# GpSimd's column sums before its squares, four result buffers, and two more maxima passes under the heads, in a fused attention and ternary-FFN kernel

## The chip, the cores and the metric

The kernel runs on one core of a Trainium2 chip. The metric is the device time of one launch in microseconds (us). One launch handles all eight sequences, weights included, from HBM to HBM.

## What is computed

Eight sequences of 512 tokens with 512 features pass through two sublayers. Cut to what matters:

```python
x = x + layernorm(attention(layernorm(x)))       # 16 heads of 32, causal, rope over the head index, softmax * 512**-0.5
x = x + layernorm(ffn(layernorm(x)))
def ffn(x):                                      # bitlinear: layer norm, then weights sign(round(w / mean|w|)) * mean|w|
    h = gelu(bitlinear(x, w_fc))                 # 512 -> 2048
    return bitlinear(h, w_proj)                  # 2048 -> 512; its layer norm needs mean and variance of h over 2048
```

The second bitlinear normalises h, row by row, over its 2048 hidden values. The kernel does this behind the product: it needs, for each token, the sum of the gelu values and the sum of their squares.

## The kernel before

**Steps.** The program is written out by hand, engine by engine, with semaphores (no scheduler). Step j (`iteration(j, prev, here, nxt, setup)`) overlaps three batches: the FFN of batch j-1 (`prev`), the attention of batch j (`here`), and the projections of batch j+1 (`nxt`). Steps 1 to 6 are "usual" and have all three; step 7 has no `nxt`; step 8 has only `prev`; step 0 prepares. Every engine runs its list strictly in order, so a wait holds all that stands behind it on that engine.

**Up phase.** TensorE (PE) makes 16 blocks of hidden values, 128 hidden features each, over 512 tokens (`up(u)`, L491). ScalarE (ACT) takes the gelu twice (L826, L827), VectorE (DVE) subtracts to get a low half (`hidden_low`, L1119); the block then stands as two f16 tiles, hT HI and hT LO. Between them stand passes of maxima (`max_pass`, L536, four matmuls with 1280 columns in all; `maxima` on DVE, L1124): one pass per head of the attention gives the row maxima for the softmax. `MAX_AT` puts ten passes in the up phase of their own step, `STEP_MAX` puts six in the heads of the step before.

**Sums.** `hidden_sums(u)` (L501, matmuls at L507) follows two blocks behind: eight matmuls of one column against ones add the block's gelu values over partitions into columns 264 to 267 of the PSUM bank `pv`. GpSimd (POOL) makes the squares in `squares(u)` (L1507): hi + lo (L1521), times itself (L1523), added to `acc` (L1526), block by block. `square_sums` (L513, matmuls at L518) adds `acc` over partitions with four matmuls in float32 (eight records), ahead of the weighing of head 6 (`SQUARES_AT`).

**Down product.** `ffn_down(tb, part)` (L522, L531) is the second product for 128 tokens (tb) and a quarter of the hidden values (part), eight matmuls of 512 columns. All of tb 0 comes ahead of the heads, (1, 0) behind the weighing of head 0, the others by `DOWN_AT` inside the heads.

**Heads.** In head h PE makes, in this order, queries and keys of the next batch (`QK_AT`, L487), pieces of the down product, `scores(h + 1)` (L554), a maxima pass where `STEP_MAX` has one, and `weigh(h)` (L581, 20 matmuls at L594), the product of probabilities and values. ACT takes exponentials (L868, L870), DVE their low half (`probs_low`) and `head_output(h)` (L1259: L1264, L1266, L1271). `weigh(h)` waits for the low halves of head h and for `pv` to be read (`pv_drained`).

**Finish.** For each tb DVE takes the down product out of PSUM (`final`, L1198) into one of two buffers `xn[:, tb % 2, :]`, makes moments, POOL raises to the power -1/2 (`power`, L1497), ACT normalises (`final` on ACT, L873, at the heads of `FINISH_AT`), POOL adds the residual (`finish`, L1541), SyncE stores. `hidden_mean` (L1177) and `hidden_variance` (L1185) on DVE read the two sums from `pv`.

Behind the heads comes the tail (attention's output projection, its layer norm, the turned inputs of the next up phase).

## Time and profile before

| | |
|---|---|
| median of 3 runs | 1301.1 us (1300.71 to 1302.18) |
| the profiled execution, its own time | 1301.28 us |
| its span (first to last instruction) | 1299.5 us |
| PE busy | 1183.3 us (91%) |
| DVE busy | 996.2 us (77%) |
| ACT busy | 763.5 us (59%) |
| POOL busy | 563.7 us (43%) |
| mean granted TensorE clock | 0.97 |

The time of the profiled execution is 1.8 us more than its span; sums below are made against 1301.28 us. The usual steps repeat to a hundredth of a microsecond: the first `up` of step 3 starts at 511.61 us and that of step 4 at 659.20 us, a period of 147.59 us. Times in the rows are counted from the start of the span. A row of the timeline stands for one or more like instructions in a row; its start is the start of the first.

### The profile page before, as it was taken

The page shows a single profiled execution, that of the slowest core. Times are in us where ns is not written, and L with a number is a line of the kernel's source. Part 1 is how long each engine was busy: PE and PEld are TensorE (multiplying, and loading weights), DVE is VectorE, ACT ScalarE, POOL GpSimd, SP SyncE. Part 2 cuts the span into 40 slices and gives each one's busy share as a digit, 9 for nine tenths or more (in the row PEclk, how much of TensorE's full clock was granted, in tenths as well). Part 3 has the DMA queues.
Part 4 walks back from the last instruction along what each step waited for, and adds up shares of the span by engine and source line. Part 5 has one row for each costly group of instructions (what it writes and reads, how often), then busy time and mean ns, then how long its engine had stood idle before and what let it go on. Part 6 is the DMA issues. An engine that isn't in the chain of part 4 may idle for free.

```text
span 1299.5 us, 24731 instructions
## 1 busy us (share of the span) xinstructions
PE 1183.3 (91%) x9300; PEld 647.9 (50%) x9300; DVE 996.2 (77%) x2892; ACT 763.5 (59%) x1406; POOL 563.7 (43%) x630
## 2 busy tenths in 40 slices
PE   6867789999999999999999999999999999988697
PEld 5224444555545554555545554555545554555343
DVE  4587977968787887968887887968888787867634
ACT  4628645666466755666465755666466754576390
POOL 1150603961269213971259312971159412881250
PEclk9896889999999999999999999999999999998899
DMA  8340221012300231012300222002300212000100
GB/s 333 73 154 2 50 82 34 2 25 66 106 1 3 58 89 51 2 26 66 106 1 2 58 63 77 1 20 68 110 1 3 56 43 66 1 3 18 49 1 32
DMA packets 47613, 65.08 MB, mean 50 GB/s; under 512 B 8548, under 2 KB 33156, under 8 KB 46086
## 3 DMA queue, kind: packets, MB, share of 16 engines
q1 hardware_dynamic: 47494, 63.51, 16.5%
q8 instruction: 73, 1.20, 0.4%
q14 instruction: 46, 0.38, 0.1%
HBM read 29.63 MB, written 8.39 MB: 29 GB/s over the span
## 4 chain that ended last, share of the span: by engine, by line
PE 52%; DVE 32%; ACT 11%; issue 3%; POOL 3%; DMA 0%; DVEq 0%; POOLq 0%; ACTq 0%
PE gen L487 19%; PE down L531 15%; DVE score L1139 8%; PE pv L594 4%; DVE hT L1031 4%; PE score L557 4%; DVE probs L1031 2%; PE gen L548 2%; DVE gen L1139 2%; PE score L569 1%; POOL rstd L1497 1%; DVE mx L1139 1%; DVE qkn L1244 1%; DVE bn L1170 1%; ACT qkn L808 1%
## 5 line engine op out<-in xcount | busy, mean ns | idle before, releaser
L1497 POOL TENSOR_TENSOR rstd<-veps,mhalf 128x1 f32<-128x1 f32 (+1 forms) x104 | 67.0, 645 | 501.8 <-DVE veps L1219 355.0
L868 ACT ACTIVATE probs<-score 128x512 f16<-128x512 f32 x360 | 189.2, 526 | 117.6 <-PE score L557 117.6
L487 PE MATMUL gen<-x2T,t1T 128*128 128x512 f16 x1024 | 241.9, 381 | 4.0 <-ACT x2T L807 2.5
L1031 DVE TENSOR_TENSOR probs<-score,probs 128x512 f16<-128x512 f32 x360 | 199.3, 595 | 51.3 <-ACT score L870 51.0
L531 PE MATMUL down<-t2T,hT 128*128 128x512 f16 x960 | 220.7, 381 | 0.2 <-DVE xn L1203 0.2
L870 ACT ACTIVATE score<-score 128x512 f32<-128x512 f32 x360 | 191.9, 533 | 0.0
L487 PE MATMUL gen<-xT,wa 128*128 128x512 f16 x768 | 181.9, 389 | 4.3 <-DVE mx L1139 4.3
L1031 DVE TENSOR_TENSOR hT<-gen,hT 128x512 f16<-128x512 f32 x160 | 108.4, 685 | 63.7 <-ACT gen L827 25.2
L487 PEld LDWEIGHTS gen<-x2T,t1T 128*128 128x128 f16 x1024 | 95.2, 98 | 108.9 <-ACT x2T L807 5.2
L826 ACT ACTIVATE hT<-gen,gam 128x512 f16<-128x512 f32 x128 | 88.0, 688 | 95.8 <-PE gen L487 95.7
L1139 DVE CUSTOM_DVE_ANT_0 score<-score,mask_rows 128x512 f32<-128x512 f32 (+3 forms) x312 | 143.1, 520 | 0.0
L531 PEld LDWEIGHTS down<-t2T,hT 128*128 128x128 f16 x960 | 90.5, 98 | 98.9 <-issue 2.3
L1526 POOL TENSOR_TENSOR acc<-acc,acc_add 128x512 f32<-128x512 f32 x105 | 133.2, 1268 | 8.2
L1521 POOL TENSOR_TENSOR acc_add<-hT 128x512 f32<-128x512 f16 x105 | 121.3, 1155 | 14.5 <-POOL acc L1526 0.4
L487 PEld LDWEIGHTS gen<-xT,wa 128*128 128x128 f16 x768 | 73.1, 100 | 89.9 <-issue 9.6
L1523 POOL TENSOR_TENSOR acc_add<-acc_add 128x512 f32<-128x512 f32 x105 | 109.3, 1041 | 8.2
L594 PE MATMUL pv<-v_sb,probs 128*128 128x65 f16 x2560 | 101.3, 195 | 9.6 <-DVE oA L1266 9.6
L594 PEld LDWEIGHTS pv<-v_sb,probs 128*128 128x128 f16 x2560 | 95.8, 99 | 17.6 <-DVE probs L1031 13.4
L487 PE MATMUL gen<-wa,xT 128*128 128x512 f16 x384 | 91.7, 388 | 3.7 <-DVE mx L1139 3.7
L1139 DVE CUSTOM_DVE_ANT_0 gen<-gen,mask_rows 128x512 f32<-128x512 f32 x200 | 91.8, 521 | 0.0
L557 PE MATMUL score<-qk 98*128 98x128 f16 x840 | 89.9, 246 | 0.0
L827 ACT ACTIVATE gen<-gen,gam 128x512 f32<-128x512 f32 x128 | 84.1, 657 | 0.0
(146 smaller groups left out, 1782.8 us busy)
## 6 DMA issues: line engine op xcount, KB each, us to landing
qk<-qkn SPq DMA_DIRECT2D x360, 64.0 KB, 2.0
xo<-x SPq DMA_DIRECT2D x8, 1024.0 KB, 5.4
hT<-x SPq DMA_DIRECT2D x8, 1024.0 KB, 6.4
out<-xn SPq DMA_DIRECT2D x32, 256.0 KB, 2.2
hT<-w_fc SPq DMA_DIRECT2D x4, 1024.0 KB, 15.8
hT<-w_down SPq DMA_DIRECT2D x4, 1024.0 KB, 5.5
t2T<-w_qk SPq DMA_DIRECT2D x2, 1024.0 KB, 8.5
probs<-w_v SPq DMA_DIRECT2D x1, 1024.0 KB, 10.8
```

The costliest lines, as they stand in the source:

```text
L487: mm = nc.tensor.matmul(bank[:, :], a, b, start=(start and n == 0), stop=(stop and n == len(pairs) - 1))
L531: mm = nc.tensor.matmul(bank[:, :], hT[:, half, u, PARTS * tb:PARTS * (tb + 1)], t2T[:, u, :], start=(u == 0 and half == HI), stop=(u == F ...
L557: return nc.tensor.matmul(bank[:, at:at + t1 - t0], qk[0:98, 1, h, PARTS * s:PARTS * (s + 1)], qk[0:98, 0, h, t0:t1], start=start, stop=Tr ...
L594: mm = nc.tensor.matmul(pv[:, VW * tb:VW * (tb + 1)], probs[:, h % 2, half, at:at + PARTS], v_sb[:, s, h, :], start=(s == 0 and half == HI ...
L826: nc.scalar.activation(hT[:, HI, u, :], bank[:, :], ACT.Gelu, scale=gam[:, 0:1])
L868: nc.scalar.activation(probs[:, h % 2, HI, 512 * i:512 * i + n], bank[:, 0:n], ACT.Exp, scale=1.0 / S_UP)
L870: nc.scalar.activation(bank[:, 0:n], bank[:, 0:n], ACT.Exp, scale=1.0 / S_UP).then_inc(exp_full, 1)
L1031: return V.tensor_tensor(out, whole, hi, ALU.subtract)
L1139: op = V.tensor_tensor_reduce(part, part, mask_rows[:, T - n:T], 1.0, -3.0e38, ALU.add, ALU.max, mx[:, TB * u + tb:TB * u + tb + 1])
L1521: P.tensor_tensor(whole[:, :], hT[:, HI, u, :], hT[:, LO, u, :], ALU.add).then_inc(sq_step, 1)
L1523: P.tensor_tensor(whole[:, :], whole[:, :], whole[:, :], ALU.mult).then_inc(sq_step, 1 if u else 2)
L1526: P.tensor_tensor(acc[:, :], acc[:, :], acc_add[:, :], ALU.add).then_inc(sq_step, 1)
```

## The change

It does the following in the steps with `prev` and `here` (1 to 7). Step 8 keeps `hidden_sums` and the old `squares`.

1. PE's `hidden_sums` is left out. POOL adds hi and lo of each block and adds that to a new tile `acc_sum`; the first two blocks are also squared in passing (`BOTH`). The squares of the other 14 blocks come behind the last sum, and need hi + lo once more. In place of `hidden_sums` stands `value_sums`: four float32 matmuls of `acc_sum` against ones, ahead of the weighing of head 0, which wait for all of POOL's sums.
2. `square_sums`, `hidden_variance` and the first two `final_terms` move from head 6 to head 12; the finishing of tb 0, 1 and 2 on ACT from heads 6, 9 and 13 to 13, 14 and 15.
3. Four result buffers instead of two (`result`: xn 0, xn 1, acc_sum, acc_add), each with its own semaphore; stores stand later in SyncE's list.
4. Piece (0, 3) of the down product goes behind `scores(1)`, ahead of the weighing of head 0; (1, 0) goes from behind that weighing to head 5.
5. Eight maxima passes in the heads (7 to 14) instead of six (8 to 13), eight in the up phase instead of ten. This holds for step 0 too.

```diff
-DOWN_AT = {0: [(1, 0)], 5: [(1, 1), (1, 2)], 6: [(1, 3)], 9: [(2, 0), (2, 1)], 10: [(2, 2), (2, 3)],
+DOWN_AT = {0: [(0, 3)], 5: [(1, 0), (1, 1)], 6: [(1, 2), (1, 3)], 9: [(2, 0), (2, 1)], 10: [(2, 2), (2, 3)],
            13: [(3, 0), (3, 1)], 14: [(3, 2), (3, 3)]}
-LAST_DOWN_AT = {h: [divmod(n + 4, 4)] for n, h in enumerate((0, 1, 2, 4, 7, 8, 9, 10, 12, 13, 14, 15))}
+LAST_DOWN_AT = {h: [divmod(n + 3, 4)] for n, h in enumerate((0, 1, 2, 3, 4, 7, 8, 9, 10, 12, 13, 14, 15))}
-SQUARES_AT = 6
-FINISH_AT = {6: 0, 9: 1, 13: 2}
+SQUARES_AT = 12
+FINISH_AT = {13: 0, 14: 1, 15: 2}
-STEP_MAX = {8: 0, 9: 1, 10: 2, 11: 3, 12: 4, 13: 5}
+STEP_MAX = {7: 0, 8: 1, 9: 2, 10: 3, 11: 4, 12: 5, 13: 6, 14: 7}
-MAX_AT = {0: 6, 2: 7, 3: 8, 5: 9, 7: 10, 8: 11, 9: 12, 10: 13, 11: 14, 12: 15}
+MAX_AT = {0: 8, 2: 9, 3: 10, 5: 11, 7: 12, 9: 13, 11: 14, 12: 15}
...
-        SQ_STEPS = 3 * FC
+        BOTH = 2
+        SUM_STEPS = 2 * FC + BOTH
+        SQ_STEPS = SUM_STEPS + 3 * (FC - BOTH)
...
+                def value_sums():
+
+                    pe.wait_ge(sq_step, SQ_STEPS * (j - 1) + SUM_STEPS)
+                    for tb in range(TB):
+                        mm = nc.tensor.matmul(pv[:, H_SUM + tb:H_SUM + tb + 1], acc_sum[:, PARTS * tb:PARTS * (tb + 1)],
+                                              ones32[:, 0:1], start=True, stop=True)
+                    mm.then_inc(hsum_full, 1)
...
                     need(pe, pv_drained, HEADS * j + h)
+                    if prev and here and h == 0:
+                        value_sums()
                     if prev and here and h == SQUARES_AT:
                         square_sums()
...
-                        if u >= 2:
+                        if u >= 2 and not here:
                             hidden_sums(u - 2)
...
+                def square_added(n):
+
+                    pool.wait_ge(sq_step, n)
+                    P.tensor_tensor(acc_add[:, :], acc_add[:, :], acc_add[:, :], ALU.mult).then_inc(sq_step, 1)
+                    pool.wait_ge(sq_step, n + 1)
+                    P.tensor_tensor(acc[:, :], acc[:, :], acc_add[:, :], ALU.add).then_inc(sq_step, 1)
+
+                def sums(u):
+
+                    n = SQ_STEPS * (j - 1) + 2 * u + (BOTH if u >= BOTH else 0)
                     pool.wait_ge(g_drained, g0 + G["up", u] + 1)
...
+                    P.tensor_tensor(acc_add[:, :], hT[:, HI, u, :], hT[:, LO, u, :], ALU.add).then_inc(sq_step, 1)
                     pool.wait_ge(sq_step, n + 1)
...
+                    P.tensor_tensor(acc_sum[:, :], acc_sum[:, :], acc_add[:, :], ALU.add).then_inc(sq_step, 1)
+                    if u < BOTH:
+                        square_added(n + 2)
...
                 for u in range(FC if prev else 0):
-                    squares(u)
+                    if here:
+                        sums(u)
+                    else:
+                        squares(u)
                     if nxt and u == 2:
                         power(LX, slice(0, TB), j + 2, j + 2)
+                for u in range(BOTH, FC if prev and here else 0):
+                    squares(u)
```

How the lists change at three places. First PE in a usual step, from the last blocks of the up phase to the weighing of head 0 (`up` writes gen<-x2T,t1T; the sums are pv<-ones; scores are score<-...; weighing is pv<-v_sb,probs). Before:

```order
L487 MATMUL gen<-x2T,t1T 128x512 x8
L507 MATMUL pv<-ones,hT 128x1 x8
L482 MATMUL gen<-ident,xn 128x128 x4
L531 MATMUL down<-t2T,hT 128x512 x16
L507 MATMUL pv<-ones,hT 128x1 x16
L569 MATMUL score<-mask_b,identb 128x512
...
L531 MATMUL down<-t2T,hT 128x512 x16
L569 MATMUL score<-mask_b,identb 128x512
...
L594 MATMUL pv<-v_sb,probs 128x65 x20
L531 MATMUL down<-t2T,hT 128x512 x8
```

Now:

```order
L500 MATMUL gen<-x2T,t1T 128x512 x16
L495 MATMUL gen<-ident,xn 128x128 x4
L554 MATMUL down<-t2T,hT 128x512 x16
L592 MATMUL score<-mask_b,identb 128x512
...
L554 MATMUL down<-t2T,hT 128x512 x8
L592 MATMUL score<-mask_b,identb 128x512
...
L554 MATMUL down<-t2T,hT 128x512 x8
L530 MATMUL pv<-ones,acc_sum 128x1 x4
L619 MATMUL pv<-v_sb,probs 128x65 x20
```

The sums have gone from between the blocks to one place right ahead of the weighing of head 0. Then POOL at the start of a step's blocks. Before:

```order
L1521 TENSOR_TENSOR acc<-hT 128x512
L1523 TENSOR_TENSOR acc<-acc 128x512
L1521 TENSOR_TENSOR acc_add<-hT 128x512
L1523 TENSOR_TENSOR acc_add<-acc_add 128x512
L1526 TENSOR_TENSOR acc<-acc,acc_add 128x512
L1521 TENSOR_TENSOR acc_add<-hT 128x512
L1523 TENSOR_TENSOR acc_add<-acc_add 128x512
```

Now:

```order
L1569 TENSOR_TENSOR acc_sum<-hT 128x512
L1571 TENSOR_TENSOR acc<-acc_sum 128x512
L1576 TENSOR_TENSOR acc_add<-hT 128x512
L1578 TENSOR_TENSOR acc_sum<-acc_sum,acc_add 128x512
L1559 TENSOR_TENSOR acc_add<-acc_add 128x512
L1561 TENSOR_TENSOR acc<-acc,acc_add 128x512
L1576 TENSOR_TENSOR acc_add<-hT 128x512
L1578 TENSOR_TENSOR acc_sum<-acc_sum,acc_add 128x512
```

From block 2 on two operations a block lead to the sums, and three more a block follow behind all sums. Last DVE in head 12, after the change:

```order
L1231 SCALAR_TENSOR_TENSOR acc_sum<-c_sum,h_negm,down 128x512
L1218 TENSOR_TENSOR h_msq<-h_negm 128x4
L1220 SCALAR_TENSOR_TENSOR h_var<-pv,h_msq 128x4
L1223 TENSOR_SCALAR e_fin<-h_var,c_fin 128x4
L1247 TENSOR_TENSOR veps<-mv,e_fin 128x1 x2
L1158 COPY wait_copy<-mhalf 128x1
L1165 ISA gen,mx<-gen,mask_rows 128x512
```

The variance, which waits for the weighing of head 12 itself, now stands ahead of that head's maxima; before, it stood in head 6, which has no maxima.

## Rows read from the trace of the kernel before

**Rows 1.** The page: the chain that ended last, by engine

```profile
PE 52%; DVE 32%; ACT 11%; issue 3%; POOL 3%; DMA 0%; DVEq 0%; POOLq 0%; ACTq 0%
```

**Rows 2.** Timeline of PE, up phase of step 3: start us, us, instruction

```profile
525.18 0.35 PE L507 MATMUL pv<-ones,hT 128*128 128x1 f16 x8
525.39 0.70 PE L548 MATMUL score<-qk 96*128 96x512 f16 x4
525.93 1.89 PE L487 MATMUL gen<-x2T,t1T 128*128 128x512 f16 x8
```

**Rows 3.** Timeline of POOL, blocks 0 to 3 of step 3

```profile
517.03 1.15 POOL L1521 TENSOR_TENSOR acc<-hT 128x512 f32<-128x512 f16 x1 [7.78 <-DVE hT L1031]
...
519.51 1.15 POOL L1521 TENSOR_TENSOR acc_add<-hT 128x512 f32<-128x512 f16 x1
520.74 1.04 POOL L1523 TENSOR_TENSOR acc_add<-acc_add 128x512 f32<-128x512 f32 x1
521.85 1.27 POOL L1526 TENSOR_TENSOR acc<-acc,acc_add 128x512 f32<-128x512 f32 x1
523.27 1.15 POOL L1521 TENSOR_TENSOR acc_add<-hT 128x512 f32<-128x512 f16 x1
...
526.99 1.02 POOL L1497 TENSOR_TENSOR rstd<-veps,mhalf 128x4 f32<-128x4 f32 x1
...
528.25 1.15 POOL L1521 TENSOR_TENSOR acc_add<-hT 128x512 f32<-128x512 f16 x1
```

**Rows 4.** Timeline of PE, step 3: weighing of heads 0, 6, 7, 8, 11, 12

```profile
560.61 0.77 PE L594 MATMUL pv<-v_sb,probs 128*128 128x65 f16 x20
...
586.54 1.02 PE L518 MATMUL pv<-ones,acc 128*128 128x1 f32 x8 [0.16 <-issue]
587.43 0.76 PE L594 MATMUL pv<-v_sb,probs 128*128 128x65 f16 x20
...
591.39 0.78 PE L594 MATMUL pv<-v_sb,probs 128*128 128x65 f16 x20
...
596.45 0.77 PE L594 MATMUL pv<-v_sb,probs 128*128 128x65 f16 x20
...
612.73 0.77 PE L594 MATMUL pv<-v_sb,probs 128*128 128x65 f16 x20
...
618.26 0.77 PE L594 MATMUL pv<-v_sb,probs 128*128 128x65 f16 x20
```

**Rows 5.** Timeline of DVE, step 3: heads 1, 6 and 14

```profile
569.96 1.28 DVE L1271 TENSOR_TENSOR xo<-oA,r_sum 128x128 f32<-128x128 f32 x1
...
588.23 0.16 DVE L1190 TENSOR_TENSOR h_msq<-h_negm 128x4 f32<-128x4 f32 x1 [1.39 <-PE pv L594]
...
588.96 1.61 DVE L1031 TENSOR_TENSOR probs<-score,probs 128x512 f16<-128x512 f32 x3
...
629.45 0.69 DVE L1031 TENSOR_TENSOR probs<-score,probs 128x512 f16<-128x512 f32 x1 [1.29 <-ACT score L870]
```

**Rows 6.** One DVE line, whole run: ns minimum, median, maximum

```profile
L1271 DVE TENSOR_TENSOR xo<-oA,r_sum x128: 292/293/1394, 117.1 to 1205.4; 128x128 f32<-128x128 f32 x128
```

**Rows 7.** Windows in step 7: busy us (count) of PE, PEld, DVE, ACT, POOL; PEclk

```profile
1163.80:1167.30 3.50, 1.91 (x28) 1.40 (x28) 3.37 (x7) 3.50 (x9) 2.32 (x3) 0.85 0.01 2
1167.30:1170.70 3.40, 2.37 (x20) 2.27 (x20) 2.01 (x6) 2.23 (x6) 0.00 (x0) 0.50 0.00 0
1170.70:1174.10 3.40, 3.40 (x24) 1.67 (x22) 2.54 (x9) 0.81 (x1) 0.74 (x3) 0.65 0.00 0
```

**Rows 8.** Timeline of PE, step 7: weighing of head 0, square sums, head 12

```profile
1147.23 0.78 PE L594 MATMUL pv<-v_sb,probs 128*128 128x65 f16 x20
...
1168.46 1.84 PE L518 MATMUL pv<-ones,acc 128*128 128x1 f32 x8 [1.03 <-DVE probs L1031]
...
1193.81 0.77 PE L594 MATMUL pv<-v_sb,probs 128*128 128x65 f16 x20
```

**Rows 9.** Timeline of POOL, step 7: block 0

```profile
1107.38 1.15 POOL L1521 TENSOR_TENSOR acc<-hT 128x512 f32<-128x512 f16 x1 [7.78 <-DVE hT L1031]
```

More of the change, by code:

```diff
@@ L267, in build, with result @@
         y_banks = (*score, pv)
-        SQ_STEPS = 3 * FC
+        BOTH = 2
+        SUM_STEPS = 2 * FC + BOTH
+        SQ_STEPS = SUM_STEPS + 3 * (FC - BOTH)
+        def result(tb, here):
+            return (xn[:, 0, :], xn[:, 1, :], acc_sum[:, :], acc_add[:, :])[tb if here else tb % 2]
         def down_bank(tb, here):
@@ L417, in iteration @@
                 for g in range(4):
+                    if g == 3 and prev and here:
+                        store(0)
+                        store(1)
                     if g == 3 and here:
@@ L424, in iteration @@
                         sp.dma_start(xres, x_v[:, bass.ds(row, TB), :]).then_inc(xres_in, 16)
+                    if g == 3 and prev and here:
+                        store(2)
                     if nxt:
@@ L427, in iteration @@
                     if prev:
-                        for tb in ((), (0, 1), (2,), (3,))[g]:
+                        for tb in (((), (), (), (3,)) if here else ((), (0, 1), (2,), (3,)))[g]:
                             store(tb)
             run(sp, iteration)
-            for half in stored:
-                sp.wait_ge(half, 16 * 2 * BATCHES)
+            for done in stored:
+                sp.wait_ge(done, 16 * BATCHES)
         @block.tensor
@@ L528, in ffn_down @@
                     bank = down_bank(tb, here)
+                    if tb == 0 and here:
+                        drained("up", 4 * part + 3)
                     for u in range(4 * part, 4 * part + 4):
@@ L740, in iteration @@
                     ffn_down(0, 1)
-                    hidden_sums(FC - 2)
-                    hidden_sums(FC - 1)
+                    if not here:
+                        hidden_sums(FC - 2)
+                        hidden_sums(FC - 1)
                 if here:
@@ L755, in iteration @@
                         queries_keys(*QK_AT[h])
-                    pieces = (DOWN_AT if nxt or not here else LAST_DOWN_AT).get(h, ()) if prev else ()
-                    if h:
+                    pieces = (DOWN_ALONE if not here else DOWN_AT if nxt else LAST_DOWN_AT).get(h, ()) if prev else ()
+                    if h or not here:
                         for tb, part in pieces:
@@ L764, in iteration @@
                             values(0)
+                        if h == 0 and pieces:
+                            ffn_down(*pieces[0])
                         if setup and h == 2:
@@ L769, in iteration @@
                         weigh(h)
-                    if h == 0 and pieces:
-                        ffn_down(*pieces[0])
                 if here:
@@ L1373, in iteration @@
                         x_low(X_AT[u])
-                if prev:
+                if prev and not here:
                     hidden_mean()
-                    if not here:
-                        hidden_variance()
+                    hidden_variance()
                 if here:
@@ L1382, in iteration @@
                     x_low(3)
-                if prev:
+                if prev and not here:
                     final(0)
                     final_moments(0)
-                    if not here:
-                        final_terms(0)
-                        finish(0)
+                    final_terms(0)
+                    finish(0)
                 final_at = FINAL_AT if nxt or not here else LAST_FINAL_AT
```

59 lines of the change are left out of this document (38 added, 21 removed).

## The prediction

> **What bounds the kernel now.** I read the chain of waits first. More than half of it is PE, then DVE [rows 1]; POOL has 3% of it, so POOL is free as long as what it makes comes in time. The timeline of one usual step comes next, since steps 1 to 6 repeat. In the up phase PE goes from one group to the next without a gap: a group of the hidden sums takes 525.39 - 525.18 = 0.21 us, a maxima pass 525.93 - 525.39 = 0.54 us [rows 2]. So what is removed there from PE is removed from the step, if nothing else becomes late. POOL's timeline shows what could: its operations stand back to back from 517.03 us on, and block 2 begins at 523.27 us, 3.76 us behind block 1 [rows 3]. At present nobody notices, because their result is wanted only in head 6, at 586.54 us [rows 4]. The change wants a result of POOL in head 0. That is where I look.
>
> **The change, part by part** (step 3 stands for the usual ones, times from the rows).
>
> *Removed from PE:* 16 groups of hidden sums, 16 x 0.21 = 3.4 us. Moved out of the up phase: two passes, 2 x 0.54 = 1.1 us. Head 0 has the same three quarters and one more quarter of the down product ahead of its weighing as before, so PE comes to that place at 560.61 [rows 4] - 3.4 - 1.1 = 556.1 us.
>
> *When POOL's sums are ready.* Intervals between starts [rows 3]: block 0 (hi + lo, square) 519.51 - 517.03 = 2.48. Block 1: hi + lo 1.23, add to acc_sum 1.35 (1.27 and the gap of 0.08 that stands behind an operation of its kind), square 1.11, add to acc 1.42; 5.11 in all. Blocks 2 to 15: 14 x (1.23 + 1.42) = 37.1. The two power operations between them take 528.25 - 526.99 = 1.26. Less the last gap, 0.15, that makes 45.8 us, all POOL's own work: blocks from PE come every 2.3 us or faster and are not what it waits for. The sums end at 517.03 + 45.8 = 562.8 us. **PE waits there for 562.8 - 556.1 = 6.7 us.** The value sums take what the square sums take, 587.43 - 586.54 = 0.9 us [rows 4], so the weighing of head 0 starts at 563.7 us instead of 560.61: **+3.1 us a step**. The piece (1, 0) behind it only moves to head 5, still in the heads, so nothing is gained back. The 4.5 us that PE saved lie inside the wait: how fast the up phase becomes no longer counts. What waits behind PE is everything: queries and keys, scores 2, ACT's exponentials and DVE behind them.
>
> *Two passes more in the heads.* Head 6 to 7, with queries and keys and no pass, takes 591.39 - 587.43 = 3.96 us; to head 8, the first with a pass, 596.45 - 591.39 = 5.06; between two such heads 618.26 - 612.73 = 5.53 [rows 4]. Head 7 becomes the first kind (+1.1) and head 8 the second (+0.5): **+1.6**.
>
> *Heads 12 to 14.* In head 12 DVE now waits for the weighing before it takes the maxima. In head 6 the variance and its term held DVE from 588.23 to 588.96, and DVE had waited for the weighing [rows 5]. In head 12 the maxima begin some 1 us later against the weighing, and heads 13 and 14 have maxima and final moments, so DVE has no slack to catch up until head 14, where it now has 1.29 us of idle time [rows 5]. The change fills that with another pass, 0.54 on PE and about three times as much on DVE. I take 0.54 + 1.06 = **+1.6**; bounds 0.6 (PE's pass alone) and 2.2. ACT's finishing of tb 2 stands ahead of the tail's first copies, but the later weighing of head 15 hides it; without that cover it would cost about 1.
>
> *POOL busy until head 11 instead of head 3.* DVE's L1271 takes 292 ns as a rule but up to 1394 ns [rows 6]. One of 1.28 us stands in head 1 [rows 5], while POOL still makes squares (517.03 + 2.48 + 15 x 3.76 + 1.26 = 577.2). With POOL busy, heads 7, 8 and 11, where the chain of maxima and queries leaves little slack, each lose 0 to 0.5: I take **+0.8**, bounds 0 and 1.6. The Trainium skill ("SBUF — State Buffer", who interferes with whom) says that of DVE and GpSimd the later one is blocked for the other's whole instruction; the trace agrees, with 1394 against 292 ns.
>
> *The clock.* In step 7 PE was busy 1.91 of 3.50 us, and the granted clock then fell to 0.50 of full [rows 7]; the square sums in that spell took 1.84 instead of 1.02 us [rows 8, 4]. That is 1.2 GHz instead of 2.4. The slow spell lasted (0.15 x 3.5 + 0.5 x 3.4 + 0.35 x 3.4) / 0.5 = 6.8 us. A wait of 6.7 us with PE wholly idle is emptier than what came before it there, so I expect such a spell in every step, over work that is PE's own. Half of the spell is lost, but only of that part which lies behind the wait: between 0 (it lies all inside, or doesn't come) and 3.4; I take **+2.2**, two thirds, since the fall comes while PE still waits. The Trainium skill ("TensorE: Matmul & The Clock Gate", what's actually happening) says that the throttled 1.2 GHz is the default and that sustained work alone frees it; the trace agrees, with 0.50 behind the thin stretch. Were that rule wrong here, the sum would be without this term.
>
> *Sum of a usual step:* 3.1 + 1.6 + 1.6 + 0.8 + 2.2 = 9.3 us; six of them 56 us.
>
> *Step 7* (no projections, so a step in which the heads are light on PE). Sums end at 1107.38 [rows 9] + 45.8 - 1.26 (no power operations) = 1151.9. Squares of 14 blocks behind them, 3.76 each [rows 3], end at 1204.5. PE's heads 0 to 12 took 1193.81 - 1147.23 = 46.6 us with more pieces in them [rows 8], so from 1152.8 it comes to the square sums by 1199 at the latest and **waits again**. The weighing of head 12 starts at 1204.5 + 0.9 = 1205.4 instead of 1193.81: +11.6, and with the clock at half behind a wait and the finishing crowded into heads 13 to 15 I take +14 (bounds 11.6 and 16).
>
> *Step 0* gets the two passes in heads 7 and 14 too: 1.1 (as head 7 above) and about 0.9: +2. *Step 8* keeps its lists: 0. The stores and the load of x for the residual stand later on SyncE's queue; the first residual sum is some 16 us behind head 14, so I cost them at nothing. If that cover were gone, DVE's first_sum would wait. The four result buffers remove no wait that the rows show.
>
> In all 56 + 14 + 2 = 72 us, on the profiled execution's 1301.3: 1373 us. The median is 1301.1, the same to 0.2.
>
> **Rivals.**
> 1. *The sums come in time* (the other side). If an add pair on POOL took 2.17 us instead of 2.65, they would end at 556.1. Then a usual step has -3.4 - 1.1 + 0.9 + 1.6 + 0.6 = -1.4 and the kernel about 1290 us. Against it: POOL's operations vary by hundredths in these rows and the new add has the shape of L1526. It decides at 556.1 us. Chance 0.04.
> 2. *The clock holds*, or its loss is hidden: 6 x 2.2 and about 2 of step 7 less, 1358 us. For it: steps 1 to 6 have short waits only and nothing in them shows a full stop. Against: rows 7. Chance 0.15.
> 3. *The squares are late in usual steps too.* They end at 562.8 + 52.6 = 615.4; PE comes to head 12 at 563.7 + 57.65 - 0.9 = 620.5 (618.26 - 560.61 = 57.65 before, with the square sums in it). 5 us of cover, more with the half clock. If DVE holds POOL for much longer than in these rows, say 8 us, 3 us are paid in each step: 1391 us. Chance 0.10.
>
> **How the numbers follow.** My forecast has 0.68, the rivals 0.29, and 0.03 is left for what I don't see, half of it near no change. Lower end: without clock and port and with the small bound in heads 12 to 14, 6 x (3.1 + 1.6 + 0.6) + 11.6 = 43, 1345 us. Upper end: 6 x (3.1 + 1.6 + 2.2 + 1.6 + 3.4) + 16 + 3 = 90, 1392 us; it takes in rival 3. Only rival 1 and part of the rest lie outside. Changes under 0.2%, 2.6 us, can't be told from none. Faster 0.04, the same 0.02, slower 0.94.
>
> **What would show it.** Right: before the value sums PE idle for 6 to 7 us in each usual step, released by POOL's add to acc_sum; POOL's sum phase 45.8 us long; a granted clock of 0.5 behind it; a second wait of 5 us or more before the square sums of step 7; a period of 157 us instead of 147.59. Wrong: if the value sums wait under 1 us, the theory falls; if the period is near 155, the clock term is wrong; if PE waits in head 12 of usual steps, rival 3 holds.

## The result, and the profile after

| | before | after |
|---|---|---|
| median | 1301.6 us (1300.71 to 1302.18, 4 runs) | 1376.4 us (1374.68 to 1378.85, 4 runs) |
| ratio | | 1.0574 (1.0553 to 1.0594) |
| span of the profiled execution | 1299.5 us | 1377.0 us |
| mean granted clock | 0.97 | 0.95 |
| period of a usual step | 147.59 us | 157.05 us |
| step 7, first `up` to first `up` of step 8 | 128.9 us | 144.0 us |

The kernel became 5.7% slower; 1373 us was forecast. The page of the changed kernel, its busy times and its chain by engine, against [rows 1]:

```profile
PE 1202.3 (87%) x8460; PEld 641.6 (47%) x8460; DVE 1015.7 (74%) x2892; ACT 761.7 (55%) x1406; POOL 808.6 (59%) x833
...
PE 41%; DVE 32%; POOL 14%; ACT 9%; issue 4%; DMA 0%; POOLq 0%; DVEq 0%; ACTq 0%
```

POOL has gone from 3% of the chain to 14%, and PE has lost what it gained. PE's timeline in step 3, from its first `up` at 536.15 us to the weighing of head 0 (start us, us, instruction):

```profile
544.70 0.39 PE L571 MATMUL score<-qk 96*128 96x512 f16 x1 [0.82 <-DVE mx L1165]
...
552.28 1.90 PE L500 MATMUL gen<-x2T,t1T 128*128 128x512 f16 x8 [0.43 <-DVE hT L1057]
...
557.71 1.90 PE L500 MATMUL gen<-x2T,t1T 128*128 128x512 f16 x8 [0.68 <-DVE hT L1057]
...
582.14 1.89 PE L554 MATMUL down<-t2T,hT 128*128 128x512 f16 x8
...
587.27 1.84 PE L530 MATMUL pv<-ones,acc_sum 128*128 128x1 f32 x8 [3.24 <-POOL acc_sum L1578]
588.97 1.26 PE L619 MATMUL pv<-v_sb,probs 128*128 128x65 f16 x20
```

The new wait is there, 3.24 us before the value sums. Ahead of it PE's waits for DVE in this stretch add up to 3.9 us, against 1.6 us in the kernel before: freed of the hidden sums, it waits for DVE to empty banks. POOL in the same step, against [rows 3]:

```profile
541.57 1.15 POOL L1569 TENSOR_TENSOR acc_sum<-hT 128x512 f32<-128x512 f16 x1 [7.78 <-DVE hT L1057]
...
585.87 1.26 POOL L1578 TENSOR_TENSOR acc_sum<-acc_sum,acc_add 128x512 f32<-128x512 f32 x1
587.21 1.15 POOL L1553 TENSOR_TENSOR acc_add<-hT 128x512 f32<-128x512 f16 x1
```

Its sum phase is 587.21 - 541.57 = 45.6 us long, without a gap, and ends 51.1 us after the step's first `up`. The windows around the wait (busy us of PE, PEld, DVE, ACT, POOL, then the granted clock), against [rows 7]:

```profile
583.20:586.80 3.60, 0.83 (x4) 0.20 (x2) 1.03 (x3) 0.86 (x3) 3.34 (x3) 0.96 0.00 0
586.80:590.20 3.40, 2.93 (x29) 2.93 (x30) 0.00 (x0) 0.00 (x0) 3.17 (x4) 0.50 0.02 5
590.20:593.60 3.40, 3.40 (x11) 1.16 (x9) 3.04 (x6) 0.00 (x0) 3.17 (x4) 0.54 0.00 0
593.60:597.00 3.40, 3.40 (x39) 2.14 (x38) 1.74 (x4) 2.56 (x5) 3.16 (x4) 1.00 0.00 0
```

After 3.2 us without work PE gets half the clock, 1.2 GHz, for 6.8 us, of which 0.8 us lie inside the wait and the rest behind it. The value sums take 1.84 us in it. All six usual steps have such a spell.

The weighings of heads 11 to 14, and the square sums in their new place in head 12, against [rows 4]:

```profile
644.33 0.77 PE L619 MATMUL pv<-v_sb,probs 128*128 128x65 f16 x20
...
649.86 1.00 PE L539 MATMUL pv<-ones,acc 128*128 128x1 f32 x8
650.72 0.76 PE L619 MATMUL pv<-v_sb,probs 128*128 128x65 f16 x20
...
656.48 0.77 PE L619 MATMUL pv<-v_sb,probs 128*128 128x65 f16 x20
...
661.85 0.77 PE L619 MATMUL pv<-v_sb,probs 128*128 128x65 f16 x20
```

No wait stands before 649.86: in usual steps the squares are in time. In step 7 they are not, as PE's timeline there shows; a third wait, in head 1, is one that I had not looked for:

```profile
1214.31 1.84 PE L530 MATMUL pv<-ones,acc_sum 128*128 128x1 f32 x8 [8.23 <-POOL acc_sum L1578]
...
1219.94 3.59 PE L554 MATMUL down<-t2T,hT 128*128 128x512 f16 x8 [2.67 <-DVE xn L1231]
...
1266.07 1.84 PE L539 MATMUL pv<-ones,acc 128*128 128x1 f32 x8 [2.57 <-POOL acc L1561]
```

And DVE's normalising product, whose usual 0.29 us [rows 6] became 0.35 in the median and 1.40 at most, ahead of the weighing of head 10. The first row is of DVE's timeline, the second of POOL's:

```profile
637.70 1.40 DVE L1299 TENSOR_TENSOR xo<-oA,r_sum 128x128 f32<-128x128 f32 x1
...
637.68 1.27 POOL L1561 TENSOR_TENSOR acc<-acc,acc_add 128x512 f32<-128x512 f32 x1
```

POOL's operation began first and ended at 638.95; DVE's, begun 0.02 us later, ended at 639.10, 0.15 us behind that. All 50 of these products that took over 0.6 us in this trace ended 0.15 us behind the POOL operation that they met. This is the case that the Trainium skill ("SBUF — State Buffer", who interferes with whom) describes: the one that comes later is blocked for the whole instruction of the other.

**Where a usual step's time lies**, in this kernel and in seven of the experiments below. Each stretch is the difference of two starts in PE's timeline of a middle step; w0 to w15 are the weighings of heads 0 to 15:

| | up to w0 | w0 to w1 | w1 to w6 | w6 to w8 | w8 to w11 | w11 to w15 | w15 to next | period |
|---|---|---|---|---|---|---|---|---|
| before | 49.00 | 5.69 | 21.13 | 9.02 | 16.28 | 19.29 | 27.18 | 147.59 |
| after | 52.82 | 6.04 | 21.56 | 10.94 | 16.82 | 21.70 | 27.17 | 157.05 |
| sums_later | 47.70 | 3.96 | 22.37 | 11.24 | 16.29 | 21.70 | 27.19 | 150.45 |
| busy_wait | 51.93 | 3.96 | 21.56 | 11.45 | 16.29 | 21.70 | 27.18 | 154.07 |
| passes_back | 52.13 | 5.60 | 21.57 | 9.85 | 16.28 | 20.53 | 27.94 | 153.90 |
| late_and_passes | 48.47 | 3.96 | 22.76 | 9.03 | 17.25 | 20.54 | 27.90 | 149.91 |
| passes_alone | 48.64 | 5.70 | 21.12 | 11.22 | 16.29 | 20.46 | 27.15 | 150.58 |
| late_squares_alone | 49.70 | 3.97 | 21.55 | 9.02 | 16.28 | 20.55 | 27.93 | 149.00 |
| no_sums | 47.79 | 5.69 | 21.12 | 9.03 | 16.28 | 19.29 | 27.18 | 146.38 |

Square sums and value sums stand ahead of the weighing of their head, so they count to the stretch that ends there. The piece of the down product that the change takes from head 0 to head 5 is worth 1.73 us in the second column.

### The profile page after: what moved, and what is told of

Its sections match the earlier page's. It is cut to its first block, busy times and chain, and to the rows that moved or that the text cites. A ratio compares the mean times of both kernels' runs of the same rounds, so it can differ in the third digit from the quotient of the medians.

```text
span 1377.0 us, 23266 instructions
## 1 busy us (share of the span) xinstructions
PE 1202.3 (87%) x8460; PEld 641.6 (47%) x8460; DVE 1015.7 (74%) x2892; ACT 761.7 (55%) x1406; POOL 808.6 (59%) x833
## 4 chain that ended last, share of the span: by engine, by line
PE 41%; DVE 32%; POOL 14%; ACT 9%; issue 4%; DMA 0%; POOLq 0%; DVEq 0%; ACTq 0%
PE gen L500 18%; PE down L554 8%; POOL acc_sum L1578 4%; DVE gen L1165 4%; POOL acc_add L1576 4%; DVE score L1165 4%; DVE probs L1057 3%; PE pv L619 3%; DVE hT L1057 3%; PE score L580 2%; DVE xo L1299 2%; DVE qkn L1272 2%; PE gen L571 1%; POOL acc L1561 1%; POOL rstd L1532 1%
## 5 line engine op out<-in xcount | busy, mean ns | idle before, releaser
L554 PE MATMUL down<-t2T,hT 128*128 128x512 f16 x960 | 223.8, 385 | 3.8 <-DVE xn L1231 3.1
L500 PE MATMUL gen<-xT,wa 128*128 128x512 f16 x768 | 192.2, 405 | 8.8 <-DVE mx L1165 8.7
L1578 POOL TENSOR_TENSOR acc_sum<-acc_sum,acc_add 128x512 f32<-128x512 f32 x105 | 132.8, 1265 | 8.2
L1576 POOL TENSOR_TENSOR acc_add<-hT 128x512 f32<-128x512 f16 x105 | 121.1, 1153 | 14.3 <-POOL acc L1571 1.0
L834 ACT ACTIVATE qkn<-gen,qk_bias 128x512 f16<-128x512 f32 x60 | 41.2, 686 | 141.7 <-PE gen L500 141.7
L1553 POOL TENSOR_TENSOR acc_add<-hT 128x512 f32<-128x512 f16 x98 | 113.0, 1153 | 7.7
L1165 DVE CUSTOM_DVE_ANT_0 score<-score,mask_rows 128x512 f32<-128x512 f32 (+3 forms) x256 | 117.3, 519 | 0.0
L1165 DVE CUSTOM_DVE_ANT_0 gen<-gen,mask_rows 128x512 f32<-128x512 f32 (+3 forms) x256 | 117.3, 519 | 0.0
L619 PE MATMUL pv<-v_sb,probs 128*128 128x65 f16 x2560 | 105.0, 198 | 8.7 <-DVE oA L1294 8.5
L619 PEld LDWEIGHTS pv<-v_sb,probs 128*128 128x128 f16 x2560 | 100.0, 102 | 17.4 <-DVE probs L1057 12.7
```

The costliest lines, as they stand in the source:

```text
L500: mm = nc.tensor.matmul(bank[:, :], a, b, start=(start and n == 0), stop=(stop and n == len(pairs) - 1))
L554: mm = nc.tensor.matmul(bank[:, :], hT[:, half, u, PARTS * tb:PARTS * (tb + 1)], t2T[:, u, :], start=(u == 0 and half == HI), stop=(u == F ...
L619: mm = nc.tensor.matmul(pv[:, VW * tb:VW * (tb + 1)], probs[:, h % 2, half, at:at + PARTS], v_sb[:, s, h, :], start=(s == 0 and half == HI ...
L1165: op = V.tensor_tensor_reduce(part, part, mask_rows[:, T - n:T], 1.0, -3.0e38, ALU.add, ALU.max, mx[:, TB * u + tb:TB * u + tb + 1])
L1553: P.tensor_tensor(acc_add[:, :], hT[:, HI, u, :], hT[:, LO, u, :], ALU.add).then_inc(sq_step, 1)
L1576: P.tensor_tensor(acc_add[:, :], hT[:, HI, u, :], hT[:, LO, u, :], ALU.add).then_inc(sq_step, 1)
```

## The experiments

My theory was the prediction's: the value sums come late, the clock falls behind that wait, the two passes and the crowded heads 12 to 14 cost the rest. Rivals: the wait is a symptom and something else is as long; the clock does not matter; the passes or the late squares are free.

**1. The value sums taken where they are ready** (`sums_later`).

```diff
+VALUES_AT = {True: 2, False: 0}
-                    if prev and here and h == 0:
+                    if prev and here and h == VALUES_AT[nxt]:
                         value_sums()
```

The mean and the first final piece on DVE go with it.

> The change with the value sums (and hidden_mean and final of tb 0) taken ahead of the weighing of head 2 instead of head 0 in steps 1 to 6. Theory (PE waits for POOL's sums in head 0, and the clock falls behind it): the wait goes, since head 2 comes later than the sums; head 0 is weighed near 48 us after the step's first up instead of 52.8, the 2.1 us lost at half clock go too, the value sums cost 0.9 later: -6 us a step, near 1340 us. Rival (the shared port and the passes under the heads are the cost, the wait only shows where PE has slack): the wait turns up elsewhere, 1370 us or more.

Measured: 1338.0 us (1337.64 to 1338.44, 2 runs), ratio 1.0281 (1.0251 to 1.0311) to before. PE's timeline in step 3, weighing of head 0, value sums and weighing of head 2:

```profile
570.16 0.77 PE L620 MATMUL pv<-v_sb,probs 128*128 128x65 f16 x20
...
578.10 0.95 PE L531 MATMUL pv<-ones,acc_sum 128*128 128x1 f32 x8
578.91 0.76 PE L620 MATMUL pv<-v_sb,probs 128*128 128x65 f16 x20
```

Half of the loss, 38 of 75 us, hangs on that wait and the clock behind it, in steps 1 to 6. The sums in head 2 cost their own 0.8 us and nothing else, at full clock. But up to w0 the step is only 1.3 us shorter than before, although PE has 3.4 us of sums and 1.1 us of passes less to do there.

**2. The same wait, filled with matmuls nobody needs** (`busy_wait`).

```diff
                 def value_sums():
+                    for i in range(14 if nxt else 36):
+                        nc.tensor.matmul(pv[:, :], t1T[:, i % EC, 0:PARTS], x2T[:, HI, i % EC, :], start=True, stop=True)
                     pe.wait_ge(sq_step, SQ_STEPS * (j - 1) + SUM_STEPS)
```

> The change with 14 matmuls of 512 columns (36 in step 7) into the free bank pv ahead of the wait for the value sums; their result is overwritten. They are 3.0 us of work inside a wait of 3.3. Theory (the idle PE loses its clock, worth 0.8 us on the value sums and 2.1 us behind them): granted clock stays at 1.0 there, step shorter by 2.9 us, 7.8 in step 7 at most; near 1355 us. Rival (the clock costs nothing on this path): 1376 us, the same.

Measured: 1358.0 us (1357.6 to 1358.39, 2 runs), ratio 1.0434 (1.0404 to 1.0464). PE's timeline in step 3, and the window that holds it:

```profile
575.34 3.19 PE L529 MATMUL pv<-x2T,t1T 128*128 128x512 f16 x14
578.66 1.05 PE L532 MATMUL pv<-ones,acc_sum 128*128 128x1 f32 x8
579.58 0.77 PE L621 MATMUL pv<-v_sb,probs 128*128 128x65 f16 x20
```

```profile
574.00:578.00 4.00, 4.00 (x20) 1.83 (x19) 1.70 (x3) 1.53 (x4) 3.70 (x4) 1.00 0.00 0
578.00:582.00 4.00, 3.86 (x40) 2.42 (x39) 1.38 (x4) 0.00 (x0) 3.77 (x4) 1.00 0.00 0
```

POOL's sums end no sooner, and yet a step is 3.0 us shorter: 0.9 in the value sums, 2.1 between w0 and w1. This is the clock alone, 18 us of the 75; from w6 to w11 the step is as long as in the changed kernel (27.74 against 27.76 us).

**3. Six passes in the heads again** (`passes_back`).

```diff
-STEP_MAX = {7: 0, 8: 1, 9: 2, 10: 3, 11: 4, 12: 5, 13: 6, 14: 7}
+STEP_MAX = {8: 0, 9: 1, 10: 2, 11: 3, 12: 4, 13: 5}
-MAX_AT = {0: 8, 2: 9, 3: 10, 5: 11, 7: 12, 9: 13, 11: 14, 12: 15}
+MAX_AT = {0: 6, 2: 7, 3: 8, 5: 9, 7: 10, 8: 11, 9: 12, 10: 13, 11: 14, 12: 15}
```

> The change with ten maxima passes in the up phase and six in the heads, as before. Theory (the up phase is hidden behind POOL's sums, so passes there are free, and two passes in the heads cost 3.5 us a step with their chains): head 0 is weighed at the same 52.8 us, heads shorter by 3.5 us a step, step 0 by some us; near 1352 us. Rival (the passes in the heads fill DVE's and PE's slack, and DVE is then late in the up phase): 1370 us or more, with head 0 later than 52.8.

Measured: 1356.7 us (1354.91 to 1358.52, 2 runs), ratio 1.0424 (1.039 to 1.0459). The step is 3.15 us shorter. The up phase did not become longer by its two passes, since they run inside the wait. But 1.1 of the 3.15 us stand up to w0 (0.7) and from w0 to w1 (0.4), and they are the clock's: PE's timeline and its windows in step 3,

```profile
578.66 1.02 PE L530 MATMUL pv<-ones,acc_sum 128*128 128x1 f32 x8 [2.60 <-POOL acc_sum L1578]
```

```profile
578.20:581.60 3.40, 2.94 (x31) 2.29 (x32) 0.65 (x3) 0.00 (x0) 3.17 (x4) 0.73 0.02 5
581.60:585.00 3.40, 3.40 (x17) 1.52 (x15) 2.41 (x5) 0.41 (x1) 3.16 (x4) 0.77 0.00 0
```

Behind the shorter wait of 2.60 us the slow spell is 3.4 us long in steps 2 to 5, where it begins 0.6 to 1.4 us after the value sums do, and 6.9 us long in steps 1 and 6. The other 2.0 us stand behind w6.

**4. The kernel before without its sums on PE** (`no_sums`): only the last block is summed.

```diff
                 def hidden_sums(u):
+                    if here and u < FC - 1:
+                        return
```

> The kernel before with hidden_sums of blocks 0 to 14 left out in steps 1 to 7 (the mean of the hidden values is wrong); nothing is put in their place. It shows what removing them from PE is worth at most. If PE bounds the up phase: 15 x 0.21 x 7 = 22 us less, 1279 us. Theory by now (DVE holds PE in the up phase as soon as the sums are gone): about 1 us a step, near 1294 us.

Measured: 1290.4 us (1289.3 to 1291.58, 2 runs), ratio 0.9915 (0.9886 to 0.9944). Windows over the up phase of step 3, of the kernel before and of this one:

```profile
511.61:559.60 47.99, 46.43 (x348) 24.07 (x349) 40.19 (x132) 29.77 (x48) 39.17 (x36) 1.00 0.01 2
```

```profile
508.30:556.00 47.70, 45.44 (x237) 20.88 (x238) 39.81 (x133) 29.95 (x49) 38.95 (x35) 1.00 0.01 2
```

All of the sums' 3.2 us taken away buy 1.2 us a step. The other 2.0 us can be found in PE's timeline of step 3. Its named waits for DVE are 0.7 us longer than in the kernel before, and six of the ten passes now take 0.67 to 0.85 us from their start to that of the next work, not 0.54, which makes 1.3 us. One of them (in the kernel before 0.70 [rows 2]):

```profile
533.83 1.01 PE L550 MATMUL score<-qk 96*128 96x512 f16 x4
```

The waits inside a pass are too short for the view to name. So 1.2 us is all that the change could have won by taking the sums off PE.

**5. Both parts taken back at once** (`late_and_passes`: the edits of 1 and 3).

> The changed kernel with both parts taken back that were tried alone: value sums at head 2 (alone 1338.0 us) and six maxima in the heads as before (alone 1356.7 us). If the two parts are separate, as my theory has it, the time is near 1319 us (1315 to 1324): the usual step is about 148 us, that is the 147.6 us of the kernel before, with the work for the squares in heads 12 to 14 paid by TensorE's relief from the sums, and nearly all that is left over the kernel before is its last full step, 15 us longer. Rival: they overlap, because the clock at half after the wait is counted in both: then 1328 us or more. A second rival: the ten maxima of the up phase cost their whole matmul time there again, 1.1 us a step: 1327 us.

Measured: 1332.4 us (1329.41 to 1335.4, 2 runs), ratio 1.0235 (1.0203 to 1.0267). **A miss**: the passes, worth 3.15 us a step beside the wait, are worth 0.54 without it. Both rivals had part of it: 1.1 of the 3.15 us was the clock behind the wait, counted in both runs (experiment 3), and the passes cost time in the up phase again. The table has the rest. The two passes now cost 0.8 up to w0, as no wait covers them; the tail is 0.7 longer, as in the other two kernels with the late squares and six passes; 0.4 is lost in head 4, where DVE is late with block 0's final piece behind it, and 1.0 before head 11, where POOL's squares still run. DVE's product there (0.29 us by itself) and PE's wait behind it:

```profile
615.33 1.07 DVE L1300 TENSOR_TENSOR xo<-oA,r_sum 128x128 f32<-128x128 f32 x1
```

```profile
617.12 0.28 PE L572 MATMUL gen<-qk 96*128 96x256 f16 x1 [0.89 <-DVE qkn L1273]
```

**6. The squares cut to one column** (`short_squares`; blocks 2 to 15, the variance is left out with them).

```diff
-                    P.tensor_tensor(acc_add[:, :], hT[:, HI, u, :], hT[:, LO, u, :], ALU.add).then_inc(sq_step, 1)
-                    square_added(n + 1)
+                    P.tensor_tensor(acc_add[:, 0:1], hT[:, HI, u, 0:1], hT[:, LO, u, 0:1], ALU.add).then_inc(sq_step, 1)
+                    square_added(n + 1, 1)
```

> The changed kernel with GpSimd's squares of blocks 2 to 15, behind the value sums, cut from 512 columns to one (the variance is then not that of all columns; the waits, the order and the instruction counts stay). My theory: GpSimd at work beside VectorE in heads 0 to 11 costs about 0.9 us a step (VectorE's normalising product at 0.35 to 1.4 us instead of 0.29; the stretch before head 11 is 6.06 us instead of 5.53), and in the last full step the second wait of 2.6 us and its slow clock go: together some 11 us, about 1365 us (1361 to 1369), with the period near 156.1 us. The excess of heads 12 to 14 (1.55 us) stays, as it comes from VectorE's final pieces there. Rival: that excess is GpSimd's doing too: then 1355 us or less, period 154.6 us or less. Other rival: the port costs TensorE nothing: 1371 us or more, period 157.

Measured: 1366.3 us (1363.05 to 1369.46, 2 runs), ratio 1.0495 (1.0462 to 1.0529). All normalising products of the run in one row:

```profile
L1299 DVE TENSOR_TENSOR xo<-oA,r_sum x128: 291/293/1234, 115.6 to 1267.1; 128x128 f32<-128x128 f32 x128
```

The median is 0.29 us again, the stretch before head 8 falls from 5.90 to 5.53 us and that before head 11 from 6.06 to 5.53; those from w11 to w15 stay at 21.7 in all. So POOL beside the heads costs 0.9 us a step and has no part in what heads 12 to 14 lose. Step 7, now without a wait before its square sums, is 6.0 us shorter. The time has a third part that the edit did not aim at: the slow spell behind the value sums is 6.8 us long in four steps and 3.4 us in two, after the same wait of 3.28 us, and the two steps are 1.6 us shorter (154.9 against 156.5 us).

**7. Old sums in step 7 alone** (`seven_old`): PE sums the values there and POOL squares each block at once, with the new places of the square sums and final pieces.

```diff
-                    if prev and here and h == 0:
+                    if prev and here and nxt and h == 0:
                         value_sums()
-                        if u >= 2 and not here:
+                        if u >= 2 and not (here and nxt):
                             hidden_sums(u - 2)
...
-                    if here:
+                    if here and nxt:
                         sums(u)
+                    elif here:
+                        together(u)
```

> The changed kernel whose last full step alone (step 7) takes its sums as before: TensorE sums the gelu values in the up phase, GpSimd squares each block at once; its square sums, final pieces and maxima stay where the change put them. My theory: nearly all of that step's 15 us are the two waits (8.2 and 2.6 us), which TensorE spends without work and after which its clock is at half, less the 3.7 us of sums on TensorE that come back: the step falls from 144.0 us to about 131 (129 to 133), the time to about 1363 us. Rival: the step is longer because of the order of its down products and its final pieces in heads 13 to 15; then it keeps 137 us or more and the time is 1369 us or more.

Measured: 1357.9 us (1357.69 to 1358.0, 2 runs), ratio 1.043 (1.041 to 1.0451): 18.5 us off, more than the 13 expected. From the first `up` to w0 step 7 falls from 51.7 to 44.2 us, before the square sums no wait is left, and the half clock behind both is gone. What stays is a wait in head 1, for block 0's final piece on DVE, which the change puts behind head 0's output:

```profile
1209.77 1.90 PE L558 MATMUL down<-t2T,hT 128*128 128x512 f16 x8 [2.89 <-DVE xn L1235]
...
1248.94 0.95 PE L543 MATMUL pv<-ones,acc 128*128 128x1 f32 x8
```

**8. The kernel before with its passes beside down products** (`spread_before`).

```diff
-STEP_MAX = {8: 0, 9: 1, 10: 2, 11: 3, 12: 4, 13: 5}
+STEP_MAX = {5: 0, 6: 1, 9: 2, 10: 3, 13: 4, 14: 5}
```

> The kernel before, with its six maxima passes for the next batch only moved among the heads: from heads 8, 11 and 12, where TensorE also projects queries and keys, to heads 5, 6 and 14, where it has down products. My theory of the maxima: a pass costs TensorE its 0.54 us of matmuls where down products lie ahead of it (the stretch between two weighings is 4.83 us without a pass and 5.38 us with one), but about 1.1 us behind queries and keys (3.96 us without, 5.0 with), because its third matmul waits for VectorE to empty a general bank. Three passes moved then save about 0.5 us each, 1.6 us a step, 11 us over seven steps: about 1290 us, with a period of the steps near 146.0 us instead of 147.6. Rival: the general banks are emptied no sooner behind down products once VectorE has its final pieces in heads 13 and 14, or the passes at heads 5 and 6 wait for their stacked queries and keys: then nothing is saved, 1299 to 1305 us.

Measured: 1330.4 us (1325.72 to 1335.02, 4 runs), ratio 1.0208 (1.0184 to 1.0231). **A miss**, on the far side of both theories; my rival named the place but not the size. PE's timeline, heads 5, 7 and 9 of step 3:

```profile
595.26 0.72 PE L548 MATMUL gen<-qk 96*128 96x512 f16 x4 [1.58 <-DMA qk<-qkn]
...
603.39 4.26 PE L487 MATMUL gen<-xT,wa 128*128 128x512 f16 x12 [1.64 <-DVE mx L1139]
...
613.85 3.63 PE L531 MATMUL down<-t2T,hT 128*128 128x512 f16 x16 [0.84 <-DVE xn L1203]
```

In head 5 the pass waits for the DMA that stacks queries and keys. In head 7 PE waits for DVE and its matmuls then take 4.26 us instead of 2.75. In head 9 the down product waits for its bank, which it did not while a pass stood in head 8. The 4.26 us come from the clock. The windows of step 3 there:

```profile
601.70:605.10 3.40, 1.76 (x7) 0.61 (x6) 3.21 (x15) 1.01 (x2) 1.41 (x3) 0.70 0.36 86
605.10:608.50 3.40, 3.40 (x25) 1.78 (x24) 1.63 (x6) 0.81 (x2) 0.60 (x1) 0.80 0.46 110
```

PE has half the clock for 3.4 us from 603.1 us on, in the wait and behind it. Steps 2 to 6 all have this spell; step 1 has none and is 151.8 us long, the others 153.4 to 153.5. So 1.5 us of the 5.9 that a step loses are the clock, the rest is the waits.

**9. The passes alone, on the kernel before** (`passes_alone`: the change's two tables and nothing else).

> One part of the change alone on the kernel before: eight of the sixteen maxima in the heads instead of six (heads 7 to 14). My theory: the passes cost 1.08 us in head 7, 0.3 in head 8, and 1.2 in heads 13 and 14 (the stretches between weighings of the changed kernel against those of the run with only the passes taken back, and before), 2.6 us in all; two passes fewer in the up phase give back some 1.1 us of TensorE and leave the rest to VectorE: net 1 to 1.6 us a step, a period of 148.6 to 149.2 us, 1308 to 1312 us. Rival: the up phase is so full that TensorE and VectorE are both relieved there, and the moves cancel: 1299 to 1303 us. The other way: the passes cost 2.8 us a step as they did within the changed kernel: 1320 us.

Measured: 1321.7 us (1319.57 to 1326.18, 4 runs), ratio 1.0154 (1.013 to 1.0178). **A miss for my theory; the other way that I had named, 1320, has the right number.** The up phase gives back only 0.36 us a step, not 1.1, and head 7 costs 1.7, not 1.1; in the heads the passes cost 3.4 us in all, not 2.6. In head 7 PE waits longer for DVE than in the changed kernel, since DVE's product meets the finishing add of POOL, which the old order has in that head (rows of PE, DVE and POOL):

```profile
607.15 0.28 PE L548 MATMUL gen<-qk 96*128 96x256 f16 x1 [1.02 <-DVE qkn L1244]
```

```profile
605.23 1.20 DVE L1271 TENSOR_TENSOR xo<-oA,r_sum 128x128 f32<-128x128 f32 x1
```

```profile
605.02 1.27 POOL L1541 TENSOR_TENSOR xn<-xn,x 128x512 f32<-128x512 f32 x1 [0.93 <-ACT xn L875]
```

**10. The late squares and finishes alone** (`late_squares_alone`: sums, squares and six passes as before; square sums in head 12, finishes in heads 13 to 15, four result buffers, the down pieces as in the change).

```diff
-SQUARES_AT = 6
-FINISH_AT = {6: 0, 9: 1, 13: 2}
+SQUARES_AT = 12
+FINISH_AT = {13: 0, 14: 1, 15: 2}
```

> The other part alone: sums as before (TensorE the values, GpSimd each square at once) and six maxima as before, in all steps, but the square sums at head 12, the finishes in heads 13 to 15, a result buffer for each block, block 0's last down part at head 0. My theory of the 1.55 us that heads 12 to 14 lose in the changed kernel: they come from VectorE's two more final pieces there and from two passes; without the passes about 0.8 us a step is left (square sums 0.86 us at head 12 instead of 0.43 at head 6, +0.4 at head 13, +0.3 and -0.3 after it), five us in six steps, and step 7 gains 2.6: a period near 148.4 us and 1303.5 us (1300.5 to 1306). Rival: the late squares are what costs in those heads whatever else is there: 1.5 us a step or more, 1308 us or more. Other rival: GpSimd's work beside heads 0 to 11 was all of it: then the late order is free and 1299 us or less results.

Measured: 1309.2 us (1308.52 to 1311.49, 5 runs), ratio 1.0057 (1.0038 to 1.0076). **A miss for my theory** (1303.5 us, at most 1306); the time is in the first rival's range, but not for its reason. A step is 1.4 us longer. From w11 to w15 it loses 0.4 beside the square sums themselves. Up to w0 it loses 0.7, since the second block of scores now comes one piece sooner and waits for DVE. The moved piece and the square sums together give 0.4 back, as in the changed kernel. The theory did not have the 0.7, nor another 0.75 in the tail behind w15. Rows of ACT and of PE in the tail of step 3 show the 0.75:

```profile
637.84 0.81 ACT L904 ACTIVATE acc_sum<-acc_sum,shift,rstd 128x512 f32<-128x512 f32 x1 [2.21 <-POOL shift L1538]
...
639.68 2.76 PE L504 MATMUL score<-wp,hT 128*128 128x512 f16 x12 [0.37 <-ACT hT L836]
```

The weighing of head 15 starts at 635.94. The projection starts 3.74 us behind it, in the kernel before 3.10: 0.3 us because head 14's product takes 1.23 us on DVE beside POOL's finishing add, and 0.35 because ACT finishes tb 2 ahead of the tail's first copies. The last 0.1 us I did not find.

**11. A version that might beat both** (`last_late`): the kernel before, with the change's order of squares, final pieces and buffers in step 7 only.

```diff
-SQUARES_AT = 6
-FINISH_AT = {6: 0, 9: 1, 13: 2}
+SQUARES_AT = {True: 6, False: 12}
+FINISH_AT = {True: {6: 0, 9: 1, 13: 2}, False: {13: 0, 14: 1, 15: 2}}
```

> A version that might beat both: the kernel before in every step but the last full one (step 7); there the sums are as before too, but the square sums stand at head 12 instead of 6, the four blocks have a result buffer each, and the last part of block 0's down product is at head 0. In the run where only step 7 had its sums as before, that step took 98.2 us from its first up product to the weighing of head 15, against 101.8 us before: about 1 us of it by two maxima passes that its up phase does not have, and the rest in heads 5 to 12, where TensorE waits 1.0 us less for the squares and less for VectorE. My theory: 2.6 us saved, 1298.7 us (1297.5 to 1300), ratio about 0.998. Rival: the gain came all from the two passes fewer, which the step before pays in its heads: 1301 us or more, ratio 1.000.

Measured: 1302.6 us (1297.43 to 1304.72, 12 runs), ratio 0.9999 (0.9986 to 1.0013): no difference, the rival. Up to w0 it wins 1.1 us in step 7, and then it pays for the late final piece of block 0, in head 1 of step 7:

```profile
1149.52 2.87 PE L543 MATMUL down<-t2T,hT 128*128 128x512 f16 x8 [2.09 <-DVE xn L1221]
```

Step 7 is 1.4 us longer in the end (130.3 us against 128.9); step 0 was 1.0 us shorter in this execution, which hides most of it. No version here that computes the whole result beats the kernel before.

## Why the prediction was right

**When POOL's sums are ready: right.** 45.6 us of POOL's own work against 45.8; the value sums start 51.1 us into the step, against 562.8 - 511.61 = 51.2. Experiment 1 shows that this one dependence carries half of the loss.

**The arrival of PE at 556.1: wrong, and with it the wait of 6.7 us.** It was 3.24. I took 4.5 us of work out of PE's up phase and let PE arrive 4.5 us sooner, 44.5 us into the step; it came at 587.27 - 3.24 - 536.15 = 47.9. The sentence that failed is "what is removed there from PE is removed from the step, if nothing else becomes late". DVE, at 40.2 of 48.0 us busy, is what becomes late: the sums on PE had filled the time in which DVE empties banks, and experiments 4 and 9 measure 1.2 us for the sums and 0.36 for the passes. The 3.4 us that were missing come from three places: 2.0 from the sums, 0.7 from the passes, and 0.7 that piece (0, 3) costs behind `scores(1)` (experiment 10, up to w0). It did no harm to the forecast, because behind a wait it is the releaser that sets the time, as the prediction said itself. Rival 1 ("the sums come in time") would have been mis-sized for the same reason: 1290 us was worked out with PE's whole relief.

**+3.1 for the late sums, +2.2 for the clock: right in kind, together 5.3 against 5.9.** Up to w0 the step became 3.8 longer, 2.9 by the late sums and 0.9 by the value sums' half clock. From w0 to w1 it should have lost the piece's 1.73 us and became 0.35 longer, so the clock costs 2.1 there. In all it is 3.0 instead of 2.2, and experiment 2 gives it back exactly: 2.98. I had placed a third of the spell inside the wait; it begins nearly where the wait ends. Rival 2 ("the clock holds") would have been 1358 us, which is what the filled wait gave, to the microsecond by chance.

**Two passes in heads 7 and 8, +1.6: measured 1.9** (9.02 to 10.94 us from w6 to w8), 0.4 of it POOL's. **Heads 12 to 14, +1.6: measured 1.54** (19.29 to 21.70 from w11 to w15), with the square sums' 0.87 taken off, which the change only moves from head 6. The working was less good than the sum: the passes alone cost 1.2 there, the late squares 0.4 beside their own sums (experiments 9 and 10). **The shared port, +0.8: measured 0.9** (experiment 6), in heads 8 and 11.

**"Nothing is gained back" by moving (1, 0): wrong, by 0.4 together with the square sums.** The piece gives 1.73 between w0 and w1; w1 to w6, with the piece in it and without the square sums, became 0.43 longer, and the square sums cost their 0.87 in head 12.

**Step 7, +14: measured 15.1.** The weighing of head 12 comes 11.6 us later into the step, as forecast, since POOL's squares set it. The wait before it is 2.6 us, though, not the 5 or more that I had named as a sign: PE comes 99.2 us into the step and not by 97, as a wait in head 1 for block 0's final piece on DVE, 2.67 us, and the slow clock hold it before. I had not seen that wait. Experiment 7 shows 18.5 us hanging on the two waits, more than the whole excess, because the rest of the change, two passes fewer in the up phase among it, is then a gain of 3.5 us in this step. **Step 0, +2: too small, some 4.** The first `up` of step 1 came 5.0 us later. It varies from one execution to another, but in the six kernels with eight passes in the heads it comes at 218.6 to 224.9 us, mean 220.8, and in the seven with six at 215.4 to 218.3, mean 216.5. No run shows where in step 0 the time goes. **Step 8, 0: measured 0.2.**

The sum of usual steps was 9.3 against 9.46 a step. That is closer than the terms deserve, and partly luck: the clock came out 0.8 larger, the late sums 0.2 smaller, and the moved piece with the square sums, counted as nothing, gave 0.4 back. The parts, run alone, give 3.0 (passes) and 1.4 (late squares), and leave 5.1 for the sums on POOL with their wait and clock; taken back inside the changed kernel the passes give 3.15, of which 1.1 is the clock, and only 0.54 once the wait is gone. Terms of this kind hold against a given neighbour, not by themselves. The 0.75 us of the tail behind w15 stand in all three kernels with late squares and six passes and in none with eight. The prediction had named this cost, with "about 1", as hidden by the later weighing of head 15: with six passes head 15 follows head 14 after 3.3 us instead of 4.2, and the cover is gone. No run took ACT's finishing away, so this is read from the rows of experiment 10 and not tested by itself.

## What to carry to other kernels

When work goes from the busiest engine to a free one, first work out when the free engine is done, from its own back-to-back durations, and compare that with the place that wants the result. A result that is late by 3 us can cost more than 3 us if TensorE stands still for it, because its clock was halved behind the wait, here for 3.0 us a step; taking the result two heads later won back half of the loss. And work taken from an engine that is 97% busy is worth only what the next engine lets through, here 1.2 of 3.2 us: ask who is at 84%. And read a part's worth in the table, stretch by stretch, before adding it to another's: both can hold the same clock.
